# High part first, and one row of transposes: the order of TensorE's work in the second part of a decoder layer

## What is computed

```python
h = rmsnorm(embeds, g_res)
h = jnp.einsum('bld,ed->ble', h, W_in) + b_in
...
return depool_out + h
...
xq, xs = _mx_quantize(x2)
wq, ws = _mx_quantize(w2)
out = (xq * xs[..., None]) @ (wq * ws[..., None]).T + bias
...
x = _layernorm(x + _L0_xattn_ref(...))
x = _layernorm(x + _L0_ffn_ref(...))
```

## Time and profile before

| | |
|---|---|
| median of 3 runs | 1695.96 us (1695.05 to 1696.47) |
| the profiled execution | 1694.65 us |
| its span | 1692.9 us, granted TensorE clock 0.979 of full speed on average |
| TensorE matmul, weight load | 1607.8 us (95%), 1151.1 us (68%) |
| VectorE, ScalarE, GpSimd | 1201.1 us (71%), 1155.3 us (68%), 686.4 us (41%) |
| DMA | 95.88 MB, 57 GB/s on average |

### The profile page before, as it was taken

The page is one execution under the profiler, slowest core; times in us unless marked ns, Lnnn a source line. Parts: engine busy times, 40 slices in busy tenths (PEclk is TensorE's granted clock), DMA queues, the critical chain, the costliest instruction groups (busy, mean ns, idle before and its releaser), DMA issues. The chain is left out here.

```text
span 1692.9 us, 31914 instructions
## 1 busy us (share of the span) xinstructions
PE 1607.8 (95%) x12212; PEld 1151.1 (68%) x12212; DVE 1201.1 (71%) x1825; ACT 1155.3 (68%) x1522; POOL 686.4 (41%) x637
## 2 busy tenths in 40 slices
PE   7999999999999999999999999986589999999996
PEld 5756776676676677667667667753468877787884
DVE  6577567668757766765875776689577777877874
ACT  6696778678678777877877777784136656565664
POOL 2033115204403410530341142025368878887886
PEclk9999999999999999999999999997799999999998
DMA  5100102201200220220021022010512222222211
GB/s 166 51 26 14 63 1 76 76 1 63 88 2 2 75 76 1 76 76 2 26 77 50 2 76 76 26 50 1 167 49 81 76 81 82 81 74 81 75 38 62
DMA packets 49198, 95.88 MB, mean 57 GB/s; under 512 B 3568, under 2 KB 3888, under 8 KB 49072
## 3 DMA queue, kind: packets, MB, share of 16 engines
q1 hardware_dynamic: 38960, 76.29, 14.0%
q10 hardware_dynamic: 10112, 17.69, 2.9%
HBM read 60.38 MB, written 33.59 MB: 56 GB/s over the span
## 5 line engine op out<-in xcount | busy, mean ns | idle before, releaser
L729 DVE SCALAR_TENSOR_TENSOR feat<-feat,phases 128x1024 f32<-128x1024 f32 x256 | 301.1, 1218 | 207.4 <-ACT feat L620 207.3
L620 ACT ACTIVATE feat<-phases 128x1024 f32<-128x1024 f32 x256 | 248.4, 1024 | 141.3 <-PE phases L473 115.1
L627 ACT ACTIVATE feat<-feat 128x1024 f32<-128x1024 f32 x256 | 271.8, 1062 | 65.0 <-DVE feat L729 56.2
L373 POOL TENSOR_TENSOR xt_hi<-xt_raw,zero 128x512 fp32r<-128x512 f32 x60 | 69.9, 1194 | 532.9 <-PE bank L464 501.9
L633 ACT ACTIVATE feat<-feat 128x1024 f32<-128x1024 f32 x256 | 255.5, 1047 | 6.7 <-DVE feat L736 6.6
L736 DVE TENSOR_SCALAR feat<-feat 128x1024 int32<-128x1024 int32 x256 | 198.2, 778 | 49.1 <-ACT feat L627 48.9
L386 POOL TENSOR_TENSOR res<-res,bo_all 128x512 f32<-128x512 f32 x64 | 75.9, 1213 | 188.8 <-DMA res<-x 188.6
L561 PE MATMUL kv_sum<-feat,kv_cols 128*32 128x512 f32 x1024 | 126.5, 613 | 8.2 <-ACT feat L633 8.2
L535 PE MATMUL kv_sum<-feat,v 128*32 128x256 f32 x2048 | 123.8, 382 | 0.0
L1189 ACT ACTIVATE xs<-xs,shift,rstd 128x512 f32<-128x512 f32 x96 | 71.4, 806 | 66.9 <-POOL shift L1064 66.9
L462 PE MATMUL bank<-xt_hi,win_hi 128*128 128x512 f32 x256 | 108.8, 425 | 8.1 <-DVE win_lo L680 8.1
(11 more groups left out here) (197 smaller groups left out, 3959.2 us busy)
## 6 DMA issues: line engine op xcount, KB each, us to landing
normed<-res SPq DMA_DIRECT2D x32, 513.0 KB, 4.1
res<-x SPq DMA_DIRECT2D x32, 512.0 KB, 4.1
xt_raw<-xT SPq DMA_DIRECT2D x15, 1024.0 KB, 7.0
xs<-normed SPq DMA_DIRECT2D x24, 513.0 KB, 3.8
out<-xs ACTq DMA_DIRECT2D x24, 512.0 KB, 2.8
feat<-normed SPq DMA_DIRECT2D x8, 513.0 KB, 3.8
out<-feat ACTq DMA_DIRECT2D x8, 512.0 KB, 2.8
xt_raw<-ctx SPq DMA_DIRECT2D x8, 256.0 KB, 3.6
```

The costliest lines, as they stand in the source:

```text
L620: act.activation(feat[2 * (w % 2) + p][:, 0, :], phases[:, 2 * p:2 * p + 2, :].rearrange("p h n -> p (h n)"), ACT.Identity, bias=ROUND).th ...
L627: act.activation(f[:, 1, :], f[:, 0, :], ACT.Sin, scale=-TWO_PI).then_inc(sin_done, 1)
L729: dve.scalar_tensor_tensor(f[:, 0, :], f[:, 0, :], ROUND, phases[:, 2 * p:2 * p + 2, :].rearrange("p h n -> p (h n)"), ALU.subtract, ALU.s ...
```

## The change

It does two things, both in the second part.

A product no longer goes block by block through its three terms. `high_product` takes the eight matmuls with the high part, `low_product` the four with the low part behind them. The wait ahead of the product is now for the bank (`last_use`) and for ScalarE's high part (`hi_ready`); the wait for VectorE's low part (`bank_free` at the place of turn or back) stands between the two. The matmuls are the same in number and size. `hi_place` finds the number of a turn or back among the high parts.

The order of every full slot is changed in `slot_order`: the two turns, which stood ahead of each ffn product, stand behind both, right ahead of the back transposes. It holds for slots 6 and 7 of the first body, the loop and the last body, 26 slots. Slots 0 to 5 and the tail keep their order.

```diff
--- before.py
+++ after.py
@@ -880,12 +880,12 @@
             [("ffn", 0), ("ffn", 1), ("norms",), ("means",)],
         )[s]
     if s % PPB == PPB - 2:
-        return [("quant",), ("lin", 0), ("lin", 1), ("scale",), ("turn", 0), ("ffn", 0), ("select",), ("turn", 1), ("ffn", 1),
+        return [("quant",), ("lin", 0), ("lin", 1), ("scale",), ("ffn", 0), ("select",), ("ffn", 1), ("turn", 0), ("turn", 1),
                 ("means",), ("back", 0), ("back", 1), ("norms",)]
     if s % PPB == PPB - 1:
-        return [("quant",), ("lin", 0), ("patch",), ("lin", 1), ("count",), ("scale",), ("turn", 0), ("ffn", 0), ("choose",),
-                ("turn", 1), ("table",), ("ffn", 1), ("means",), ("back", 0), ("back", 1), ("norms",)]
-    return [("quant",), ("lin", 0), ("lin", 1), ("scale",), ("turn", 0), ("ffn", 0), ("turn", 1), ("ffn", 1), ("means",),
+        return [("quant",), ("lin", 0), ("patch",), ("lin", 1), ("count",), ("scale",), ("ffn", 0), ("choose",),
+                ("table",), ("ffn", 1), ("turn", 0), ("turn", 1), ("means",), ("back", 0), ("back", 1), ("norms",)]
+    return [("quant",), ("lin", 0), ("lin", 1), ("scale",), ("ffn", 0), ("ffn", 1), ("turn", 0), ("turn", 1), ("means",),
             ("back", 0), ("back", 1), ("norms",)]
 
 
@@ -988,6 +988,12 @@
             if step in order.full:
                 return order.place(mode, step)
             return order.place(mode, (step[0], step[1] + BODY, *step[2:]), back=1)
+
+        def hi_place(mode, step):
+
+            if step in hi_order.full:
+                return hi_order.place(mode, step)
+            return hi_order.place(mode, (step[0], step[1] + BODY, *step[2:]), back=1)
 
         def slots_of(mode):
 
@@ -1083,12 +1089,15 @@
 
         @block.tensor
         def _(pe):
-            def product(o, hi, lo, w_hi, w_lo, closed):
+            def high_product(o, hi, w_hi, w_lo):
                 for n in range(KD):
                     cols = slice(n * P, n * P + P)
                     pe.matmul(o, hi[:, cols], w_hi[:, n, :], start=(n == 0), stop=False)
                     pe.matmul(o, hi[:, cols], w_lo[:, n, :], start=False, stop=False)
-                    last = pe.matmul(o, lo[:, cols], w_hi[:, n, :], start=False, stop=(closed and n == KD - 1))
+
+            def low_product(o, lo, w_hi, closed):
+                for n in range(KD):
+                    last = pe.matmul(o, lo[:, n * P:n * P + P], w_hi[:, n, :], start=False, stop=(closed and n == KD - 1))
                 return last
 
             def body(i, mode):
@@ -1111,8 +1120,11 @@
                             last = pe.transpose(b[:, m * P:(m + 1) * P], xs[k % RING][:, t, m * P:(m + 1) * P], ident[:])
                         last.then_inc(product_done, 1)
                     elif kind == "lin":
-                        freed(last_use, place(mode, ("turn", k, t)))
-                        product(b[:], turn_hi[t], turn_lo[t], win_hi, win_lo, False)
+                        freed(last_use)
+                        wait(pe, hi_ready, i * hi_order.n + hi_place(mode, ("turn", k, t)) + 1)
+                        high_product(b[:], turn_hi[t], win_hi, win_lo)
+                        freed(place(mode, ("turn", k, t)))
+                        low_product(b[:], turn_lo[t], win_hi, False)
                         if k % PPB == 0 and t == 0:
                             pe.wait_ge(chosen_ready, batch + 1)
                             pe.wait_ge(table_ready, batch + 1)
@@ -1136,8 +1148,11 @@
                             last = pe.transpose(b[:, m * P:(m + 1) * P], scaled[k % 2][:, at:at + P], ident[:])
                         last.then_inc(product_done, 1)
                     elif kind == "ffn":
-                        freed(last_use, place(mode, ("back", k, t)))
-                        product(b[:], back_hi[t], back_lo[t], wf_hi, wf_lo, True).then_inc(product_done, 1)
+                        freed(last_use)
+                        wait(pe, hi_ready, i * hi_order.n + hi_place(mode, ("back", k, t)) + 1)
+                        high_product(b[:], back_hi[t], wf_hi, wf_lo)
+                        freed(place(mode, ("back", k, t)))
+                        low_product(b[:], back_lo[t], wf_hi, True).then_inc(product_done, 1)
 
             body(0, "first")
             with pe.Fori(1, BODIES - 1) as i:
```

## The result

The changed kernel takes 1707.41 us at the median (1705.34 to 1711.6, 4 runs), beside 1695.51 us before on the same chip (1692.08 to 1696.47, 4 runs). The ratio is 1.0077, 95% interval 1.0053 to 1.0101: slower by some 12 us (13 by the ratio, which goes by the means) where 6.7 were forecast. The median lies inside the range given, near its upper end, and 4.7 us above the forecast; the ratio, put on the 1695.96 us from which the forecast started, gives 1709.0, just beyond the range's end of 1708.5. The profiled execution took 1705.34 us, its span is 1703.6 us.

A forecast was written before the change was run, and what follows sets the result against it. TensorE's own list, 100 us busy of 100, was taken to bound the second part. 6.3 - 1.4 + 2.4 - 0.7 - 0.7 + 0.8 = +6.7 us gave a 1702.7 us median, range 1698.8 to 1708.5.

The forecast's parts named there:

- the main step: Slots 6 to 31: lin 0 waits for turn_lo on turn 0's bank; 18 plain slots +0.35 us each, +6.3 us.
- The row read off slot 4: Slot 4 of the first body before: transposes plus the wait behind them take 2.01 us, making a plain slot 13.62 us.
- Slots 10 and 18: Two slots that had a gap before the next lin 0 lose it: -0.68 us each, -1.4 us.
- the tail: Last ffn products: the split takes back_lo's 0.70 us off the chain that ends last, -0.7 us.
- Rival 2: VectorE comes late: at_end, chosen and table ahead of turn_lo hold it, adding 6 us, about 1709; chance 0.09.
- The 0.09 us for a return from transposes to a product: Plain slot before: each return from transposes to a product costs TensorE 0.09 us, three times in a slot.
- The split in slots 0 to 5: Start: two lin 0 waits shorten, one gain shows, the second goes into the wait for patch; -0.7 us (0 to -1.4).
- Rival 3: The clock falls from 0.35 us stands in each slot; a tenth of 26 slots slow is +24 us, 1727; chance 0.02.
- the steady slots: Slots 6 to 31, 26 slots in the new order: +8.1 us forecast for the stretch.
- The table slots: Six slots with count and table: 15.20 us becomes 15.6 (up to 15.70), +0.4 each, +2.4 us.
- the added wait: Loop's 16 slots: register bank wait ahead of lin 0 may issue the matmul 0.05 us later, +0.8 us (0 to 2.4).

The follow-up runs named there:

- order_alone: New slot order with the old products (three terms by block, one wait), against the kernel before: 1704.8 us median, ratio interval 1.0037-1.0065.
- shared_bank: Changed kernel, but turn 0 is written to the bank of table_sum instead of a ring bank: 1698.94 us median, slots 6 to 31 358.37 us.
- turns_between: Changed kernel's split, but both turns stand between the two ffn products: 1697.87 us median, ratio interval 0.9996-1.0014 against the kernel before.
- swap_waits: Changed kernel with the bank wait and the high-part wait exchanged ahead of lin and ffn products: 1704.71 us median.
- start_guard: Changed kernel, but lin products of pairs 0 to 2 in the first body wait for the low part first, as before: 1705.06 us median.
- const_sbuf: Changed kernel with only VectorE's small constants moved from PSUM to SBUF: 1720.86 us median, slots 6 to 31 379.56 us.
- extra_bank: Changed kernel with turn 0 in a fifth PSUM bank and the small constants moved from PSUM to SBUF: 1718.4 us median.
- between_guard: turns_between, with lin of the first three pairs waiting for the low part before the first matmul: 1696.42 us median.
- between_tail: Order of turns_between with the split in the tail alone; elsewhere products wait for the low part first: 1696.14 us median.

## Why the prediction was right and wrong

**Right: the main step.** lin 0 of the next slot falls on turn 0's bank, and turn_lo, not the split, sets when it starts. order_alone shows the loss without the split, shared_bank removes it with one bank. The row read off slot 4, 2.01 us, is what the last body has, and its slots last 13.62 us and more. Slots 10 and 18 lost their gap as said, and the tail gave 0.5 of 0.7 us. Rival 2 occurred only as a trace of itself: in the plain slots VectorE had its 0.37 us of idle time before turn_lo and no wait names at_end or table, and in the table slots, where it has none, the row is longer by 0.12 us at most (by 0.35 in slot 7 of order_alone). The 0.09 us for a return from transposes to a product was read too high, as turns_between shows, but no term of the sum uses it.

**Wrong: "The split in slots 0 to 5", -0.7 us.** The step held the wait for patch to be a cover that only swallows a gain. The stretch lost 1.65 us instead. The gain itself was about as said: 0.56 us by the split. Another 0.69 us came from a clock that rose sooner in this execution, which is luck and no part of the step. What failed is that the step did not ask what a longer wait does to the clock, and put that at nothing: it cost 2.90 us. Rival 3 had the clock, but placed it in the 26 slots behind waits of 0.35 us, where the granted clock stayed at 1.00; the earlier trace rows and the 2.4 us of the earlier trace rows were the place to look. This term is 2.35 us of the 4.0 us by which the span was missed, and the luck hid 0.7 more. That the clock fell is seen in one profile of each kernel, five of six with a wait of this length; how often it falls in the other executions was not seen.

**Wrong in size: the steady slots**, 1.8 us. The table slots took 15.70 us, the upper end given, and not 15.6; less the added wait, which the sum has by itself, that is 0.4 us for the six. The added wait cost 0.08 us a row in the loop and not 0.05, and not by its register: 12 plain slots x 0.03 is 0.4 us. The rest, 0.9 us, is plain slots of 13.72 beside such of 13.62 with the same row: in order_alone two ffn products behind one another take 5.49 us in some slots and 5.60 in others, the matmuls 0.229 or 0.234 apart at the same granted clock. The slot of the earlier trace rows was one of the short ones. What makes the difference was not found.

The tail gave 0.2 us less and the first part was 0.3 us shorter. The other 0.7 us of the 4.7 at the median: it stands 2.07 us above the profiled execution where 1.31 was assumed. swap_waits, start_guard and order_alone, with nearly the same slots, have medians of 1704.7 to 1705.1 from six runs each, so part of the 1707.4 is the scatter of four runs.

## What to carry to other kernels

Before starting a product early on one half of its input, look which bank it writes: if the engine that makes the other half still reads that bank, the early start doesn't exist. Here the order with the fewest changes between kinds of work was then the worse one. Put a product between the step that fills such a bank and the bank's next user, or give the one step a bank of its own.

When an engine gains time ahead of a wait that is not shortened as much, the wait grows; on TensorE a longer stand can cost more than was gained (2.90 us here). A handful of matmuls without use inside the wait is the cheap test for it, and in the two profiles that had them it was also the cure.

Before a gain of 1 us in one profile is put down to a change, look whether the clock rose at the same moment in both.

An experiment that moves something aside to make room needs its own control, as const_sbuf was for extra_bank.

## What the runs showed of the hardware

- In the start TensorE dropped to its lower level behind five of six waits of 3.1 to 3.2 us and three of six of 2.4, never behind the 0.2 to 0.4 us of every slot, and not behind 3.0 us filled with matmuls. The lower level lasted 3.4 us (between_guard, between_tail) or 6.8 (the others), and cost 1.57 and 2.90 us in between_guard and in the changed kernel.
- TensorE entered the second part at its lower level and rose 7.8 to 10.2 us behind the first transpose, differently from profile to profile. 1.6 us between two such moments made 0.69 us at the table matmul (34.54 and 33.85 us).
- A VectorE operation on two SBUF operands, 128x32 large, took 1.56 us on average beside GpSimd's work and ended with it; with one operand in PSUM it took 0.19. With the constants moved to SBUF, slots 6 to 31 took 11.05 us longer (379.56 against 368.51). The Trainium skill, "SBUF — State Buffer", section "Who interferes with whom", says that VectorE and GpSimd share one pair of ports, held as an exclusive lock, and that a VectorE instruction with two SBUF inputs contends with a GpSimd instruction that reads SBUF. The rows agree.
- With two waits ahead of a matmul, one of them late, the row was 0.08 to 0.10 us longer in one order of the waits than in the other; with one late wait alone it was not (order_alone).
